# Projecting z between the steps that lead to delta, B and C, with its Silu on the way out of PSUM

## What is computed

```python
xz = jnp.einsum('bld,ed->ble', x, W_in)
xp, z = jnp.split(xz, 2, axis=-1)
xpad = jnp.pad(xp, ((0, 0), (d_conv - 1, 0), (0, 0)))
xc = conv_b + sum((xpad[:, k:k + l, :] * conv_w[:, k] for k in range(d_conv)))
xc = jax.nn.silu(xc)
dbc = jnp.einsum('ble,fe->blf', xc, W_x)      # dt, B and C
delta = jax.nn.softplus(jnp.einsum('blr,er->ble', dt, W_dt) + b_dt)
dA = jnp.exp(delta[..., None] * A)
dBx = delta[..., None] * Bm[:, :, None, :] * xc[..., None]
# h = dA_t * h + dBx_t over the tokens
y = jnp.einsum('bles,bls->ble', hs, Cm) + xc * Dp
y = y * jax.nn.silu(z)
return jnp.einsum('ble,de->bld', y, W_out)
```

## Time and profile before

| | us |
|---|---|
| runs of the kernel | 873.6, 875.08, 1957.74 |
| median of these | 875.08 |
| the profiled execution | 873.29 |
| its span in the profile | 871.6 |
| TensorE busy | 775.5 |
| VectorE busy | 639.1 |
| ScalarE busy | 448.4 |
| GpSimd busy | 361.6 |

### The profile page before, as it was taken

One profiled execution on the slowest core, in us unless ns is written; L12 is line 12 of the kernel. 1 busy time (PEld: TensorE's weight loads), 2 busy tenths in 40 slices (PEclk: granted clock), 3 DMA queues, 4 the chain that ended last, 5 costly groups with the idle time before them and its releaser, 6 DMA issues. The chain is left out here.

```text
span 871.6 us, 12022 instructions
## 1 busy us (share of the span) xinstructions
PE 775.5 (89%) x4058; PEld 572.2 (66%) x4080; DVE 639.1 (73%) x1051; ACT 448.4 (51%) x952; POOL 361.6 (41%) x195
## 2 busy tenths in 40 slices
PE   6973787788977899999999999998679999999996
PEld 2421332334433488899889888987557878787976
DVE  5799999989798878775774777577467363636366
ACT  4556655676555256663662766366454151424151
POOL 9048998978776966211111121111252131313030
PEclk9996999999999999999999999999799999999999
DMA  8000000000000200110100001010121020202001
GB/s 297 6 1 1 0 1 0 0 1 0 0 1 1 97 1 25 33 42 4 47 25 25 24 26 47 1 37 19 55 91 55 19 74 18 72 18 72 18 0 49
DMA packets 10906, 28.37 MB, mean 33 GB/s; under 512 B 1649, under 2 KB 3185, under 8 KB 10737
## 3 DMA queue, kind: packets, MB, share of 16 engines
q1 hardware_dynamic: 10864, 27.86, 9.8%
HBM read 26.80 MB, written 1.05 MB: 32 GB/s over the span
## 5 line engine op out<-in xcount | busy, mean ns | idle before, releaser
L316 POOL TENSOR_TENSOR m_ring<-m_du,m_b_sb 128x1024 f32<-128x1024 f32 x64 | 152.6, 2400 | 28.3 <-ACT m_b_sb L548 25.9
L733 DVE TENSOR_TENSOR_SCAN m_ring<-ps,m_ring 128x1024 f32<-128x1024 f32 x64 | 145.3, 2281 | 4.8 <-ACT ps L580 4.5
L1003 POOL TENSOR_TENSOR a_wl<-raw,a_wh 128x1024 fp32r<-128x1024 f32 x16 | 39.9, 2495 | 236.1 <-ACT a_wh L1199 235.8
L425 PE MATMUL ps<-m_ring,ident 128*128 128x512 f32 x256 | 128.6, 618 | 0.4 <-DVE m_ring L738 0.4
L1490 POOL TENSOR_TENSOR e_wl<-raw,e_wh 128x512 fp32r<-128x512 f32 (+1 forms) x55 | 57.2, 1047 | 164.6 <-ACT e_wh L1606 89.1
L858 PE MATMUL ps<-e_rms_hi,e_wh 128*128 128x512 f32 x200 | 86.8, 434 | 4.4 <-ACT e_sg L1619 4.4
L580 ACT ACTIVATE ps<-m_delta,m_negA 128x510 f32<-128x510 f32 x128 | 82.7, 682 | 7.9 <-DVE m_ring L733 4.1
L425 PEld LDWEIGHTS ps<-m_ring,ident 128*128 128x128 f32 x256 | 51.1, 200 | 44.2 <-issue 41.0
L860 PE MATMUL ps<-e_rms_hi,e_wl 128*128 128x512 f32 x200 | 79.4, 397 | 0.0
L859 PE MATMUL ps<-e_rms_lo,e_wh 128*128 128x512 f32 x200 | 78.9, 394 | 0.0
L1619 ACT ACTIVATE e_sg<-ps 128x512 f32<-128x512 f32 x50 | 29.3, 589 | 83.6 <-PE ps L860 83.6
(11 more groups left out here) (211 smaller groups left out, 2190.2 us busy)
## 6 DMA issues: line engine op xcount, KB each, us to landing
raw<-in_expert_w SPq DMA_DIRECT2D x30, 384.0 KB, 3.0
raw<-in_attn_w SPq DMA_DIRECT2D x20, 512.0 KB, 3.4
m_first<-in_xT SPq DMA_DIRECT2D x2, 512.0 KB, 5.0
x<-in_x_tok SPq DMA_DIRECT2D x1, 1024.0 KB, 10.7
out<-hid SPq DMA_DIRECT2D x8, 128.0 KB, 2.0
m_first<-in_w_x SPq DMA_DIRECT2D x1, 512.0 KB, 7.4
m_first<-in_w_in SPq DMA_DIRECT2D x1, 512.0 KB, 8.2
raw<-in_w_out SPq DMA_DIRECT2D x1, 512.0 KB, 8.8
```

The costliest lines, as they stand in the source:

```text
L316: nc.gpsimd.tensor_tensor(split(slot(n)), du[:, pair_of(ph):pair_of(ph) + 2, halves(ph)], b_sb[:, n % B_BUFS:n % B_BUFS + 1, :].to_broadca ...
L425: nc.tensor.matmul(ps[:, Y_BANK + c, :], ident[:, :], slot(n)[:, c * HALF:(c + 1) * HALF], start=False, stop=False, skip_group_check=True) ...
L733: nc.vector.tensor_tensor_scan(slot(n), dA_of(n), slot(n), 0.0, ALU.mult, ALU.add).then_inc(scan_done, 1)
L1003: nc.gpsimd.tensor_tensor(w[1][:, j, :], raw[:, j, :], w[0][:, j, :].bitcast(F32), ALU.subtract).then_inc(w_done, 1)
```

## The change

z's four `project_in` move on TensorE from behind the pairs of delta to among the steps of `project_x`: z0 and z1 ahead of the first, z2 behind the first, z3 behind the second; `project_x` of chunks 2 and 3 follow. The numbers r change with it (z is 4 to 7, delta 8 to 11). SP issues the z half of W_in ahead of W_x and W_dt. ScalarE takes each z chunk out of PSUM with Silu in place of Copy, ahead of the next chunk's `silu_xc`, and with one more wait, that the convolution has read the tile which z overwrites. The copies leave the softplus stage, and `silu_z` with its table loads leaves the scan. VectorE's wait for it becomes one on `pair_free`, in phase 0 alone.

```diff
--- before.py
+++ after.py
@@ -191,7 +191,6 @@
     a_exp, a_ready = sem("m_a_exp"), sem("m_a_ready")
     dp_ready = sem("m_dp_ready")
     ld_xt = sem("m_ld_xt")
-    z_ready = sem("m_z_ready")
     b_ready, b_sb_ready, c_ready = sem("m_b_ready"), sem("m_b_sb_ready"), sem("m_c_ready")
     dA_ready, dbx_ready = sem("m_dA_ready"), sem("m_dbx_ready")
     dA_zeroed = sem("m_dA_zeroed")
@@ -209,7 +208,7 @@
     kept, hid_ready = sem("m_kept"), keep["hid_ready"]
     x_kept, wh_done, w_done = keep["x_kept"], keep["wh_done"], keep["w_done"]
 
-    DELTA0, Z0 = EC, 2 * EC
+    Z0, DELTA0 = EC, 2 * EC
 
 
 
@@ -257,9 +256,9 @@
         sp.dma_start(xT[:, :, HALF:], d["xT"][:, :, HALF:]).then_inc(ld_x1, 16)
         sp.dma_start(chan[:], d["chan"]).then_inc(ld_chan, 16)
         sp.dma_start(w_in[:, :, P:E_IN], d["w_in"][:, :, P:E_IN]).then_inc(ld_w1, 16)
+        sp.dma_start(w_in[:, :, E_IN:], d["w_in"][:, :, E_IN:]).then_inc(ld_w2, 16)
         sp.dma_start(w_x, d["w_x"]).then_inc(ld_wx, 16)
         sp.dma_start(w_dt, d["w_dt"]).then_inc(ld_wdt, 16)
-        sp.dma_start(w_in[:, :, E_IN:], d["w_in"][:, :, E_IN:]).then_inc(ld_w2, 16)
         sp.dma_start(w_out, d["w_out"]).then_inc(ld_wo, 16)
         sp.dma_start(x1[:], d["x_tok"]).then_inc(ld_xt, 16)
 
@@ -391,20 +390,23 @@
         pe.wait_ge(ld_w1, 16)
         for c in range(1, EC):
             project_in(c, c)
+        pe.wait_ge(ld_w2, 16)
+        for c in range(2):
+            project_in(Z0 + c, EC + c)
         pe.wait_ge(ld_wx, 16)
-        for c in range(EC):
-            project_x(c)
+        project_x(0)
+        for c in range(2, EC):
+            project_in(Z0 + c, EC + c)
+            project_x(c - 1)
+        project_x(EC - 1)
         pe.wait_ge(ld_wdt, 16)
         pe.wait_ge(dt_sb_ready, 1)
         for c in range(EC):
             pair(DELTA0 + c, [(w_dt[:, c * P:(c + 1) * P], dt)])
 
-        pe.wait_ge(ld_w2, 16)
-        for c in range(EC):
-            project_in(Z0 + c, EC + c)
         pe.wait_ge(bc_step, 5)
         pe.wait_ge(sel_ready, 3)
-        pe.wait_ge(pair_free, Z0 + EC - 1)
+        pe.wait_ge(pair_free, DELTA0 + EC - 1)
         broadcast_b(0)
         broadcast_c(0)
         for n in range(1, B_AHEAD):
@@ -511,7 +513,8 @@
         def take_z(c):
 
             act.wait_ge(pair_ready, Z0 + c + 1)
-            nc.scalar.activation(z[:, c, :], banks(ps, 2 * (c % 2), 2), ACT.Copy).then_inc(pair_free, 1)
+            act.wait_ge(conv_step, (NTAP - 1) * (c + 1))
+            nc.scalar.activation(z[:, c, :], banks(ps, 2 * (c % 2), 2), ACT.Silu).then_inc(pair_free, 1)
 
         copy_xp(0)
         copy_xp(1)
@@ -519,7 +522,9 @@
         silu_xc(0)
         copy_xp(3)
         for c in range(1, EC):
+            take_z(c - 1)
             silu_xc(c)
+        take_z(EC - 1)
         nc.scalar.preload_act_table_set("natural_log_exp_and_others")
         act.wait_ge(dt_ready, 1)
         nc.scalar.activation(dt, banks(ps, 4, 2), ACT.Copy).then_inc(dt_sb_ready, 1)
@@ -562,13 +567,9 @@
         take_v(3)
         exp_v(2)
         log_u(1)
-        take_z(0)
         exp_v(3)
         log_u(2)
-        take_z(1)
         log_u(3)
-        take_z(2)
-        take_z(3)
         copy_b(0)
         copy_b(1)
 
@@ -617,12 +618,6 @@
         act.wait_ge(delta_ready, EC)
         act.wait_ge(a_ready, 1)
         act.wait_ge(dA_zeroed, 1)
-        def silu_z(half):
-            toks = slice(half * HALF, (half + 1) * HALF)
-            act.wait_ge(pair_free, 3 * EC)
-            nc.scalar.activation(z[:, :, toks], z[:, :, toks], ACT.Silu).then_inc(z_ready, 1)
-            nc.scalar.preload_act_table_set("natural_log_exp_and_others")
-
         for n in range(UNITS):
             decay(n)
             if n >= 2 and by_pool(n - 2):
@@ -631,8 +626,6 @@
                 take_out(OUT_AFTER.index(n - B_AHEAD + 1))
             if n + 2 < UNITS:
                 copy_b(n + 2)
-            if n % (2 * NS) == 1:
-                silu_z(phase(n) // 2)
             if n in PACK_AFTER:
                 pack(PACK_AFTER.index(n))
             if n == ROOTS_AFTER:
@@ -740,7 +733,8 @@
                                     ).then_inc(hc_ready, 1)
 
         def finish_y(ph):
-            dve.wait_ge(z_ready, ph // 2 + 1)
+            if ph == 0:
+                dve.wait_ge(pair_free, DELTA0)
             for k in range(3):
                 dve.wait_ge(summed[k], 2 * (ph + 1) * NS // 4)
             for c in range(2):
```

## The result

| | before | after |
|---|---|---|
| runs, us | 873.6, 875.0, 875.08 (and 1957.74, left out) | 881.38, 881.99, 882.37, 882.86 |
| median, us | 875.04 | 882.18 |
| profiled execution, span | 873.29, 871.6 | 881.38, 879.7 |

The ratio is 1.0084, 95% interval 1.0068 to 1.0100: 0.8% slower. That is less than the 2% that the prediction takes as its bounds, but the interval leaves out 1, so the sign is clear, and it is the one that was forecast. One run of the kernel before (1957.74) and one of a later experiment, e3 (2995.92), took over twice as long as the rest and are left out of all comparisons.

A forecast was written before the change was run, and what follows sets the result against it. TensorE was taken to bound the projections, VectorE the softplus stage and scan. 873.29 + 13.01 (move) - 2.98 (Silu) = 883.3, plus 0.7 for the runs' mean, gave 884.0 us, range 880.5 to 888.5.

The forecast's parts named there:

- The move, +13.01 us: Projections on TensorE: z's 32 records at 0.429 us add 13.73 us, less 0.72 of holes, net +13.01 us.
- the holes (0.72 us): TensorE's idle among the `project_x` steps, waiting for `silu_xc`, which interleaved z could fill: 0.72 us, no more.
- No new hole: Among the interleaved projections, takes, Silus and rings cause TensorE no new wait; smallest slack claimed over 5 us.
- rival (c): Each `project_x` waits for a take and a Silu behind it: 6.2 us more, 890.2 us; chance 6%.
- z out of the softplus stage, 0: Removing z's matmuls and copies from the softplus stage gains 0, at most 4.0 us, since VectorE is late there.
- The Silu in the scan, -2.98: Removing both Silus from the scan returns VectorE's idle: 2.98 us at unit 33, 0 at unit 1.
- The sum: Whole kernel: 873.29 + 13.01 - 2.98 = 883.3 us, plus 0.7 for the mean of runs: 884.0 us.
- the base: Starting time of the kernel before: mean 874.0 us of three runs, 0.7 above the profiled 873.29.
- Rival (a), the port: Softplus stage: six VectorE operations no longer blocked by GpSimd at the shared port, 12.7 us less, 871.3; chance 4%.
- Rival (b): Scan after phase 1: another wait takes the place of the Silu's gap, no gain there, 887.0 us; chance 7%.
- Rival (d): Around the scan's start: TensorE's low clock lasts as long again, scan standing still, 5.0 us more, 889.0; chance 8%.
- Rival (e): ScalarE: a removed table load returns elsewhere, 1.28 us each, inside the range; no chance of its own.

The follow-up runs named there:

- e3: Kernel before with one z chunk of four moved ahead of the first `project_x`, by Copy, z half of W_in loaded earlier; Silus stay: 875.92 us, ratio 1.0027.
- e2: Changed kernel with z taken by Copy and both Silus with table loads back behind units 1 and 33 (the move alone): 887.19 us, ratio 1.0157.
- e5: Changed kernel run again without edit, beside many runs of the kernel before: 882.92 us against 873.3, ratio 1.0103.
- e6: Kernel before run again without edit, for a second profile and a null comparison: 873.17 us, ratio 0.9997.
- e1: Kernel before with both Silus of z and their four table loads removed, nothing in their place: 869.61 us against 873.57, ratio 0.9955.
- e7: Kernel before with one Silu of all of z behind unit 1 of the scan, none behind unit 33: 869.82 us, ratio 0.9954.
- e8: Kernel before without silu(z), as in e1, run again for its trace only: that execution took 868.11 us.
- e4: Kernel before with one Silu of all of z ahead of the first decay, none in the scan, z's projection unmoved: 869.33 us, ratio 0.9947.
- the second comparison: e5's runs of the unedited changed kernel beside more runs of the kernel before: 882.92 us against 873.3, ratio 1.0103.

## Why the prediction was right, point by point

- **The move, +13.01 us.** Right, within its rounding: 13.03 from the first copy of xp to the copy of dt (35.99 against 22.96), 13.02 in e2, and for one chunk (e3) 2.72 where the same sum gives 2.71. The step that carries it, counting the holes (0.72 us) ahead of counting the work that is to fill them (13.73), is the one to keep. The time of one step, 0.429 us a record, held in every block.
- **No new hole.** Right: no idle entry of TensorE in this stretch; rival (c) did not occur. The slack for the takes is seen as idle of ScalarE, 4.90 us ahead of the take at 38.14 and again ahead of the one at 45.01. One figure of the check is wrong by its own numbers: the smallest slack is not over 5 us. z1 is to start at 26.7 and needs the fourth chunk of xp out of PSUM at 25.6, which is 1.1 us; after, ScalarE is done with that chunk at 26.52 and z1 starts at 27.64, again 1.1. The slacks of 5 us are those of the takes and the Silus. It cost nothing here.
- **z out of the softplus stage, 0.** Right: 0.03 us. VectorE's and GpSimd's instructions there start at the same distance from the copy of dt to 0.05 us.
- **The Silu in the scan, -2.98.** The mechanism was right, the size too small: from the product to the next scan it is 4.43 us with the Silu, and 1.18 (after) or 1.36 (e5) without, so -3.07 to -3.25 at the place itself, and about -0.4 more at unit 37. Between products 1 and 2 it took 61.4 to 61.7 us with the Silu (before, e2, e3, e6) and 57.7 to 57.9 without (e1, e5, e7, e8), all with the low clock at unit 42: 3.4 to 4.0 us, and 3.5 between e1 and the kernel before. As times: 4.0 us (e1), 3.5 us (e7), 4.2 us (e4). The term was the length of VectorE's idle entry alone; the stall also left a longer wait on TensorE three units on, which that entry doesn't hold.
- **The sum.** 13.0 - 3.5 = 9.5 us by these sizes; measured +7.3 (from the ratio) in the first comparison and +9.6 in the medians of the second. The forecast of 884.0 was 1.8 us above the first result and 1.1 above the second. Of the 1.1, 0.5 is the Silu's term and 0.7 the base: 874.0, where the kernel before has 873.3 in the second comparison. The first profiled execution is 8.1 us longer in span by parts that partly cancel, the late start of 0.94 against the 1.69 of the short wait; that its time also lies in the range owes something to luck.
- **Rival (a), the port.** Did not occur: the long operations have the same lengths, and the starts among VectorE and GpSimd are where they were. Rival (b) did not: 1.18 us behind the product. Rival (d): the low clock did last longer, as it says, from about 64 to 101 us where it was from about 69 to 86 (granted clock 0.50 and 0.51 in these stretches). It cost at most 0.3 us there: from the first scan to the product of phase 0 it took 53.34 us after and 53.07 in e5, beside 53.08 before. A low clock did cost time, but at unit 42, where the prediction had not looked. Rival (e) did not: ScalarE has 946 instructions instead of 952, two Silus and four table loads fewer.

## What to carry to other kernels

Before work is moved into the waits of an engine, add the waits up and set them beside the work: three of them held 0.7 us here, for 13.7 us of matmuls, and one chunk of z already cost 2.4. Ask also what the work costs where it stands (z stood in TensorE's idle time, and taking it away gave 0.03 us), and try each half of an edit by itself: the Silu out of the scan needed no move of z, and gives 4.2 us alone where both halves together lose 7 to 10.

## What was not expected of the hardware

- The same program waits 0.92 or 2.61 us at one matmul-bound place, by the granted clock of that execution (1.00 or 0.72). With one profile on each side such a difference looks like an effect of the change; here a second profile of the changed kernel told. Work that no edit touched took 57.7, 59.1 or 60.3 us by the same measure (clock 1.00, 0.97, 0.94).
- The time at which the first result leaves TensorE varied by 1.85 us (12.87 to 14.72) over executions. The order of work behind it decides whether that is seen: the old order, bound by VectorE's and ScalarE's chain, hid starts up to 13.52 and about half of the latest (0.83 of 1.49 us seen), and the new one, packed tight on TensorE, passed all of it on (35.98 to 35.99 us from start to dt copy).
- ScalarE's two table loads around a Silu cost their 1.28 us each and no more: from the end of a load to the next instruction there were some hundredths (load at 73.88, decay at 75.18). The Trainium skill's page "ScalarE: Activation LUTs", section "What ACT_TABLE_LOAD costs", gives about 1.28 us for the load, which the trace shows, and about as much again for a drain, which no trace here shows.
